# Expert results stored in token order, read back by plain loads, with the row loads on ScalarE's queue

## The reference, cut to what matters

```python
# first mixture: 8 experts, two per token
score = relu(x @ Wr1.T + br1) @ Wr2.T + br2
mask  = the two highest scores of each token;  w = softmax(where(mask, score, -inf))
out   = sum over e of w[e] * (relu(x @ W1[e].T + b1[e]) @ W2[e].T + b2[e])
# second mixture: 16 experts, two per token, and a shared expert
scores = softmax(x @ gate_w.T);  topw, topi = top_k(scores, 2)
h = silu(x @ w1[e].T) * (x @ w3[e].T) * comb[e];  y = sum over e of h @ w2[e].T
z = (silu(x @ sw1.T) * (x @ sw3.T)) @ sw2.T
```

## Time and profile before

| | |
|---|---|
| median of 3 runs | 1690.05 us (1690.01 to 1706.47) |
| the profiled execution | 1697.83 us, of which the span is 1696.1 us |
| busy share of the span | PE 80%, PEld 56%, DVE 45%, POOL 33%, ACT 31% |
| first mixture, first matmul to last | 662.4 to 883.6 us |
| second mixture, first matmul to last | 1352.3 to 1636.2 us |
| after the last matmul | 1636.2 to 1696.1 us |

### The profile page before, as it was taken

The page is one execution under the profiler, slowest core; times in us unless marked ns, Lnnn a source line. Parts: engine busy times, 40 slices in busy tenths (PEclk is TensorE's granted clock), DMA queues, the critical chain, the costliest instruction groups (busy, mean ns, idle before and its releaser), DMA issues.

```text
span 1696.1 us, 23482 instructions
## 1 busy us (share of the span) xinstructions
PE 1351.3 (80%) x7272; PEld 947.6 (56%) x7272; DVE 763.5 (45%) x1336; ACT 528.0 (31%) x894; POOL 560.4 (33%) x622
## 2 busy tenths in 40 slices
PE   0558799999998874999974778989899899999850
PEld 0223243443444453999972745747566588888850
DVE  1386689677786742111115545364444322222212
ACT  0354467677553210333320315043150100010100
POOL 5268789676674722101016000000003400101025
PEclk9968799899898876999996677888978999999985
DMA  5064264543543118888842000000000588888843
GB/s 129 19 155 117 53 165 124 130 100 88 155 116 76 41 41 252 271 276 271 277 147 70 5 1 1 1 0 0 1 1 31 155 242 227 229 239 226 231 109 95
DMA packets 71615, 206.45 MB, mean 122 GB/s; under 512 B 11360, under 2 KB 32608, under 8 KB 66752
## 3 DMA queue, kind: packets, MB, share of 16 engines
q1 hardware_dynamic: 59648, 181.28, 38.9%
q0 software_dynamic: 11904, 24.40, 5.0%
HBM read 183.42 MB, written 22.22 MB: 121 GB/s over the span
## 4 chain that ended last, share of the span: by engine, by line
PE 44%; DMA 16%; issue 10%; DVE 10%; POOL 8%; POOLq 5%; ACT 3%; DVEq 2%; SPq 2%; ACTq 1%
PE ps L927 31%; DMA expert<-arena 13%; PE ps L1299 3%; PE ps L1058 3%; DVE arena L1626 2%; POOL arena L633 2%; DMA arena<-sorted 2%; POOL ew_in L520 2%; PE ps L1072 2%; POOL ew_out L520 2%; PE ps L1088 1%; PE ps L1291 1%; POOL x_rows L387 1%; PE ps L922 1%; ACT arena L889 1%
## 5 line engine op out<-in xcount | busy, mean ns | idle before, releaser
L1626 DVE TENSOR_TENSOR_SCAN arena<-arena,ps 128x1024 f32<-128x1024 f32 x96 | 219.5, 2287 | 38.4 <-ACT arena L782 14.5
L927 PE MATMUL ps<-arena 96*128 96x128 f32 (+1 forms) x1680 | 222.5, 289 | 8.8 <-issue 8.2
L927 PEld LDWEIGHTS ps<-arena 96*128 96x128 f32 (+1 forms) x1680 | 213.6, 191 | 13.0 <-issue 12.9
L621 POOL DMA_DIRECT2D expert<-arena x88 | 47.7, 542 | 492.7 <-DVE arena L1752 272.7
L927 PE MATMUL ps<-xTF,wreg 96*128 96x512 f32 x352 | 199.3, 712 | 8.4 <-DVE arena L1792 4.6
L478 POOL DMA_INDIRECT sorted<-x_rows,row_i x64 | 62.7, 980 | 415.0 <-DVEq L1542 396.3
L927 PE MATMUL ps<-arena,ew_in 96*128 96x128 f32 x1248 | 149.9, 278 | 8.0 <-issue 7.7
L1058 PE MATMUL ps<-arena,pick 32*128 32x512 f32 x384 | 115.8, 691 | 48.5 <-DVE arena L1626 36.5
L927 PEld LDWEIGHTS ps<-arena,ew_in 96*128 96x128 f32 x1248 | 145.5, 194 | 11.9 <-issue 11.8
L927 PE MATMUL ps<-xT,wreg 96*128 96x512 f32 (+3 forms) x296 | 133.3, 599 | 7.5 <-DVEq L1807 5.4
L520 POOL TENSOR_TENSOR ew_in<-arena 128x1024 f32<-128x1024 f32 x48 | 112.6, 2353 | 68.6 <-PE ps L1072 41.2
(11 more groups left out here) (238 smaller groups left out, 1878.6 us busy)
## 6 DMA issues: line engine op xcount, KB each, us to landing
arena<-dt SPq DMA_DIRECT2D x64, 512.0 KB, 4.7
ew_in<-in_e_in SPq DMA_DIRECT2D x24, 768.0 KB, 6.4
arena<-in_e_in SPq DMA_DIRECT2D x24, 768.0 KB, 6.0
ew_in<-dt SPq DMA_DIRECT2D x32, 512.0 KB, 4.6
ew_out<-in_e_out SPq DMA_DIRECT2D x20, 675.0 KB, 6.7
arena<-in_e_out SPq DMA_DIRECT2D x20, 675.0 KB, 6.9
ew_in<-in_e_in SPq DMA_DIRECT2D x20, 576.0 KB, 5.5
arena<-in_e_in SPq DMA_DIRECT2D x20, 576.0 KB, 5.8
```

Of the source, the lines that this page charges most:

```text
L621: pool.dma_start(expert_rows[m][ds((i * 2 + k) * P, P), :], yb[k]).then_inc(s_yo[m][k], 16)
L927: last = pe.matmul(o, lhs, rhs, start=(n == 0), stop=(n == len(pairs) - 1))
L1626: ve.tensor_tensor_scan(hid[k % 3], dec[k % 3], bx.rearrange("p x t -> p (x t)"), 0.0, ALU.mult, ALU.add)\
```

## The change: what it does, and the diff

Each row that is scattered gets two more words: twice its token index plus 4, and its first place in the table (`x_all`, 194 words a row in place of 192). When a block's rows are loaded, VectorE works out for each of the 128 rows the row of a new table `token_rows` where its result belongs: the token's even row if this is its first place, its odd row if not, and row 2 or 3 for padding. GpSimd stores each result by an indirect DMA to those rows. It issues the stores of a pair one behind the other and then frees both buffers. The gathers go: SyncE loads each chunk of both results by one plain DMA (1536 bytes a token, 768 KB a chunk), the four directly one after the other, and signals VectorE through `s_ready`, which takes the place of `s_root` too.

The loads of a block's rows move from SyncE's list to ScalarE's (`load_row`, `first_rows`), where the two loads of the next pair stand ahead of this pair's relu or silu. SyncE waits for the scatters only after it has issued the weights of two blocks, and for the zeros not at all (ScalarE does). `route_blocks` works on 128 partitions instead of one, and its last part (`pos_i`) goes. The zeros and the blocks' first rows live in `pick`, so the memset of zeros now stands between the last scores and the last `route_picks`. GpSimd's loop over blocks is unrolled.

```diff
@@ expert_loads (SyncE)
                 sp.wait_ge(s_pos[m], 1)
-                sp.wait_ge(s_scat[m], 2 * B * 16)
-                sp.wait_ge(s_zero[m], (ne + 1) * 16)
-                with sp.Fori(0, nb // 4) as i:
+                def load_quad(i, first):
                     for j in range(4):
-                        k = j % 2
-                        sp.wait_ge(s_xbf[k], i * 2 + HALVES[m] + j // 2 + 1)
-                        sp.nop(nofuse=True)
-                        r = sp.value_load(rid[0:1, ds(i * 4 + j, 1)], min_val=0, max_val=ne * REG)
-                        sp.dma_start(xb[k], sorted_rows[m][ds(r, P), :]).then_inc(s_xb[k], 16)
+                        if first and j == 2:
+                            sp.wait_ge(s_scat[m], 2 * B * 16)
                         e = sp.value_load(eid[0:1, ds(i * 4 + j, 1)], min_val=0, max_val=ne - 1)
...
+            def token_loads(m, nb):
+                for k in range(2):
+                    sp.wait_ge(s_yo[m][k], 16 * (nb // 2))
+                for c in range(NCH):
+                    rows = token_rows[m][4 + 2 * c * CN:4 + 2 * (c + 1) * CN, :]
+                    sp.dma_start(both[:, c * CT:(c + 1) * CT, :].rearrange("p t (r d) -> p t r d", r=2),
+                                 rows.rearrange("(t p r) d -> p t r d", p=P, r=2)).then_inc(s_chunk[c], 16)
+                for c in range(NCH):
+                    sp.wait_ge(s_chunk[c], CHUNK_AT[c] + 16 * (m + 1))
+                    sp.sem_inc(s_ready, 1)
@@ scatter (GpSimd)
                 pool.wait_ge(s_row[m], n)
+                pool.tensor_scalar(x_all[:, t0:t0 + nt, D + 1:D + 2], row_f[:, 0, t0:t0 + nt]..., 0.0, None, ALU.add)
+                pool.drain()
@@ store_blocks (GpSimd); gather() goes
+                def issue(k, count):
+                    pool.wait_ge(s_yb[m], count)
+                    pool.indirect_dma_start(token_rows[m], bass.IndirectOffsetOnAxis(ids_i[k][:, 0:1], 0), yb[k], None)\
+                        .then_inc(s_yo[m][k], 16)
+                def release(k, count):
+                    pool.wait_ge(s_yo[m][k], count)
+                    pool.drain().then_inc(s_ybf[k], 1)
+                for i in range(nb // 2):
                     for k in range(2):
...
+                        issue(k, i * 2 + k + 1)
+                    for k in range(2):
+                        release(k, i * 16 + 16)
@@ ScalarE
+            def load_row(m, ne, b, k, turn):
+                act.wait_ge(s_xbf[k], turn)
+                act.nop(nofuse=True)
+                r = act.value_load(rid[0:1, b], min_val=0, max_val=ne * REG)
+                act.dma_start(xb[k], sorted_rows[m][ds(r, P), :]).then_inc(s_xb[k], 16)
+            def first_rows(m, ne):
+                act.wait_ge(s_pos[m], 1)
+                act.wait_ge(s_zero[m], (ne + 1) * 16)
+                act.wait_ge(s_scat[m], 2 * B * 16)
+                for k in range(2):
+                    load_row(m, ne, slice(k, k + 1), k, HALVES[m] + 1)
...
+            def silu_pair(i, more):
+                if more:
+                    for k in range(2):
+                        load_row(1, E1, ds(i * 2 + 2 + k, 1), k, i + HALVES[1] + 2)
                 for k in range(2):
                     act.wait_ge(s_bh[1], i * 2 + k + 1)
@@ VectorE
+            ve.memset(zero, 0.0)
             route_picks(0, E0, 3 * CT, CT)
...
+                ve.tensor_scalar(first_row[:, 0:nb], num, cst[:, C_IOTA:C_IOTA + 1], None, ALU.add)
...
+                        ve.scalar_tensor_tensor(out=ids[2 * h + k][:, :], in0=xb[k][:, D + 1:D + 2], scalar=first_row[:, ds(i * 4 + 2 * h + k, 1)],
+                                                in1=xb[k][:, D:D + 1], op0=ALU.not_equal, op1=ALU.add)
                         ve.drain().then_inc(s_xbf[k], 1)
...
                         ve.wait_ge(s_ybf[k], i * 2 + HALVES[m] + h + 1)
+                        ve.tensor_scalar(ids_i[k][:, :], ids[j][:, :], float(2 + k), None, ALU.max)
```

More of the change, by code:

```diff
@@ L69, in tower @@
         ps = ctx.enter_context(nc.psum_tensor("ps", [P, 8, 512], F32))
[L70 removed]
+        sorted_rows = [nc.dram_tensor(f"sorted{n}", (ne * REG + P, D + 2), F32, kind="Internal").ap() for n, ne in ((0, E0), (1, E1))]
         dt_rows = [nc.dram_tensor(f"dt{c}", (DG * 4, 2, 8, 2 * CN), F32, kind="Internal").ap() for c in range(NCH)]
[L72 removed]
+        token_rows = [nc.dram_tensor(f"token{n}", (2 * B * P + 4, D), F32, kind="Internal").ap() for n in range(2)]
         h_rows = sb("h_rows", [P, B, D])
[L76 removed]
+        x_all = sb("x_all", [P, B, D + 2])
+        x_rows = x_all[:, :, 0:D]
         tok_i = sb("tok_i", [P, B], I32)
@@ L145, in tower @@
         Ct = [part(23040 + 1024 * n, CN) for n in range(2)]
-        g1 = part(0, B * D).rearrange("p (t d) -> p t d", t=B)
-        g2 = part(B * D, B * D).rearrange("p (t d) -> p t d", t=B)
+        both = part(0, 2 * B * D).rearrange("p (t w) -> p t w", t=B)
         ar = mr
@@ L165, in tower @@
         QUADS, HALVES = (0, NB0 // 4), (0, NB0 // 2)
-        xb = [part(6144 + 256 * k, D) for k in range(2)]
+        xb = [part(6144 + 256 * k, D + 2) for k in range(2)]
         xbT = [part(6656 + 256 * k, 2 * P, KH).rearrange("p (k t) -> p k t", k=2) for k in range(2)]
@@ L178, in tower @@
         gate_w = sb("gate_w", [P, 2, B])
-        pos_i = sb("pos_i", [P, 2, B], I32)
+        ids = [sb(f"ids{k}", [P, 1]) for k in range(4)]
+        ids_i = [sb(f"ids_i{k}", [P, 1], I32) for k in range(2)]
         eid = sb("eid", [1, NB1], I32)
@@ L344, in expert_loads @@
                           .then_inc(s_w2[j], 16)
+                load_quad(0, True)
+                with sp.Fori(1, nb // 4) as i:
+                    load_quad(i, False)
             def store_dt(c, g):
@@ L860, in route_exp, with relu_quad @@
                 act.drain().then_inc(s_ex[m], 1)
+            def load_row(m, ne, b, k, turn):
[9 more added lines that the diff above has]
+                    load_row(m, ne, slice(k, k + 1), k, HALVES[m] + 1)
             route_exp(0, E0)
-            with act.Fori(0, NB0 // 4) as i:
+            first_rows(0, E0)
+            def relu_quad(i, more):
                 for j in range(4):
                     k, w = j % 2, e_out[0][j]
+                    if k == 0 and (more or j == 0):
+                        for n in range(2):
+                            load_row(0, E0, ds(i * 4 + j + 2 + n, 1), n, i * 2 + j // 2 + 2)
                     act.wait_ge(s_w2[j], i * 16 + 16)
@@ L871, in _ @@
                     act.drain().then_inc(s_ba[0], 1)
+            with act.Fori(0, NB0 // 4 - 1) as i:
+                relu_quad(i, True)
+            relu_quad(NB0 // 4 - 1, False)
             def shared_silu(i, f, banks):
@@ L914, in _ @@
                     act.drain().then_inc(s_bg, 1)
+            with act.Fori(0, NB1 // 2 - 1) as i:
+                silu_pair(i, True)
+            silu_pair(NB1 // 2 - 1, False)
         @block.tensor
@@ L1546, in route_blocks @@
                 ve.wait_ge(s_rank[m], n)
-                total, blocks, last, shift = rb(0, ne), rb(3, ne), rb(4, ne), rb(5, ne)
+                total, blocks, last = rb(0, ne), rb(3, ne), rb(4, ne)
                 over = rb(6, ne * B).rearrange("p (e t) -> p e t", e=ne)
@@ L1576, in route_blocks @@
                 ve.drain()
-                ve.tensor_scalar(rid[:, 0:nb], num, float(ne * REG), None, ALU.min)
+                ve.tensor_scalar(rid[:, 0:nb], num[0:1, :], float(ne * REG), None, ALU.min)
                 ve.drain().then_inc(s_pos[m], 1)
-                ve.tensor_tensor(shift, last, blocks, ALU.subtract)
+                ve.tensor_scalar(first_row[:, 0:nb], num, cst[:, C_IOTA:C_IOTA + 1], None, ALU.add)
                 ve.drain()
-                ve.scalar_tensor_tensor(out=shift, in0=shift, scalar=float(P), in1=cst[:, C_REG:C_REG + ne],
-                                        op0=ALU.mult, op1=ALU.subtract)
-                ve.drain()
-                moved = tiles_by(rb(6), 0, B, ne)
-                for r in range(2):
-                    ve.tensor_tensor(moved, tiles_by(hot_all[r][:, :], 0, B, ne),
-                                     shift.rearrange("p (a e) -> p a e", a=1).broadcast_to((P, B, ne)), ALU.mult)
-                    ve.drain()
-                    ve.tensor_reduce(rb(7, B), moved, AXX, ALU.add)
-                    ve.drain()
-                    ve.tensor_tensor(pos_i[:, r, :], rb(7, B), row_f[:, r, :], ALU.add)
-                    ve.drain()
             def route_weights(m, ne):
```

73 lines of the change are left out of this document (30 added, 43 removed).

## The result

The changed kernel takes 1646.48 us (median of 4 runs, 1641.61 to 1650.61) where the kernel before took 1692.24 beside it (4 runs, 1690.01 to 1706.47): ratio 0.9675, 95% interval 0.9625 to 0.9725 (the two medians divided give 0.973; the ratio on record weighs the runs another way). So 39 to 46 us are gained by the medians. The forecast was 61.8 of gain and 1628 us, range 1617 to 1650: right in direction, inside the range, some 18 us too good.

The account below looks back on a forecast made before the run. It took TensorE to bound the first mixture and nearly the second, and a queue of small steps the end. Terms 35.4 + 8.0 + 13 + 2.6 + 2.8 = 61.8 off 1690.05 gave 1628 us, range 1617 to 1650.

Parts of the forecast that it names:

- End: Last result to kernel end: plain chunk loads replace gathers, first sum 8.25 us after the copy; 35.4 us saved.
- middle: End of the first mixture: the same steps bring the sum forward, 8.0 us saved, bounds 0 and 9.4.
- Rival 1: The four chunk loads land together, not in turn: middle gains nothing, end 27.1, 1644.6 us; chance 0.12.
- Stores two at a time: Second mixture: paired stores leave TensorE setting the pace, 11.87 to 11.3 us a pair, 13 us saved.
- at most the 6.23: Second mixture: landing time in us of a pair's stores in flight together, within a GpSimd chain of about 9.
- Rival 2: Second mixture stays at 11.87 us a pair, held by weights, rows and indirect stores together: 1641.3 us; chance 0.15.
- Rows on ScalarE: Row loads moved to ScalarE: 2.6 us saved at the first mixture's start, 2.8 on later row loads.
- 655.1 + 4.95: First mixture's start: second row's issue time plus its landing time, giving 660.1, 1.8 us earlier.
- The lower bound written there: First mixture's start: 1.5 us lost if rows land only when both weight sets, 2.5 MB, have.
- The second mixture's start waits for the shared expert and gains nothing.: Second mixture's start: no gain from moving the row loads to ScalarE.
- ScalarE's own cost: Two row loads a pair, 2.8 us of about 11, expected covered; otherwise up to 2.8 us a pair added.
- Rival 3: Padding rows written to one of two rows take turns: 1745 us at 120 ns a write; chance 0.03.

Follow-up runs that it names:

- e8: Changed kernel with rows on SyncE, four row buffers, half a weight set ahead of first rows, VectorE writing the first place, last sums written out: 1633.33 us, ratio 0.9585.
- e11: The changed kernel itself, run again on another chip: 1663.56 us, ratio 0.9754.
- e10: Changed kernel with four row buffers on ScalarE and GpSimd's stores one by one: 1691.06 us, ratio 0.9950.
- e6: Changed kernel with four row buffers in place of two, still loaded by ScalarE: 1646.81 us, ratio 0.9661.
- e9: Kernel before with only the row loads moved to ScalarE and two weight sets early; stores one by one and gathers kept: 1702.19 us, ratio 0.9989.
- e5: Changed kernel with VectorE writing each row's first place, GpSimd's own operation and drain gone ahead of the scatter: 1651.21 us, ratio 0.9697.
- e7: Changed kernel with the eight removed VectorE operations for `pos_i` put back, their result unread: 1663.00 us, ratio 0.9787.
- e4: Changed kernel with 256 spare rows in place of two, so each padding row of a store has its own address: 1658.33 us, ratio 0.9725.
- e12: The e8 kernel run again, on the same chip as e11: 1626.38 us, ratio 0.9528.
- e3: Changed kernel with GpSimd waiting for each store and releasing its buffer before the next, still to token rows: 1688.78 us, ratio 0.9895.
- e1: Changed kernel with row loads back on SyncE in the old order, two buffers, no weight sets early: 1654.85 us, ratio 0.9732.

## Why the prediction was right and wrong

- *End, 35.4 forecast, 33.5 measured; middle, 8.0 and 8.0.* Right, with the path of the forecast: last store, chunk load, signal, 8.25 against 8.48 and 8.20. That it is so close is partly luck: the store landed in 3.27 us, not 2.3, while the wakes of GpSimd and SyncE took 0.28 and 0.06, not 0.5 each. Mis-sized: the sums, 3.2 each, come every 3.8. The 0.75 to 0.80 us between them, VectorE's loop step, had been hidden in the waits for gathers; e8, without the loop, has 3.06. Rival 1 (the chunk loads land together) is out.
- *Stores two at a time, 13 forecast.* The size was right where no row is late: the second mixture is 270.8 in e11, 13.1 under before, and e10 against e6 gives 12.2. In the first profile 4.9 was left; the late rows there account for the rest. Three sentences fell short. Stores in the first mixture "delay nobody that matters": so it was in the kernel before, where TensorE waits there for rows alone, but not once the row loads have moved (8.5 us of waiting in e9, 19.5 us in e10 against e6). The 11.87 was not the store chain's doing alone (e9). And a landing was to be "at most the 6.23": the median was 7.3, and 8 of 88 took over 9 us, which the forecast had named as a sign of being wrong; TensorE lost nothing by it that shows, other than through the rows. Rival 2, a pair held by the DMA engines together, did not come as such: e6 runs at 11.1 to 11.2 with the same bytes.
- *Rows on ScalarE, 2.6 + 2.8 forecast.* The step that failed is "655.1 + 4.95": the landing was taken from a row load that had one block's weights beside it. Beside those of four blocks, which nothing holds back any more, the loads in the chain took 10.08 and 12.93 us, and 10.99 inside the second mixture. The second row was also asked for 1.7 us later, counted from the last `row_i`, than the forecast had it, behind a zero store that took 3.42 us to land. The lower bound written there, 1.5 lost, was the right mechanism with two weight sets in place of four, and too small: 4.9 lost. Weights alone are not all of it: in e9, with its rows asked for 2.3 us sooner, the same move left the start at 23.7. What the first profile shows gained inside the first mixture, 4.3, was lost again in e11 (231.7). Alone the move gave nothing (e9). By the Trainium skill (DMA: Bandwidth & Descriptors, "Issuing engines are not separate DMA queues") that was to be expected: transfers interleave on the same engines whoever starts them. The trace agrees, with 10.99 us for a 97 KB row beside 1.5 MB of weights, and that sentence was set aside too lightly. (The sum by it is 57.7, not the 57.5 written there: 61.8 less 2.8 and 1.3.)
- *"The second mixture's start waits for the shared expert and gains nothing."* It lost 12.1, of which 5.7 is what the attention block ahead of it had gained; the two stages together went from 452.1 to 458.5, 6.4 lost. The steps missed: with the rows' issue no longer far ahead of TensorE, the scatter, the zeros and the rows' landing are next. GpSimd's small operation was costed as hidden by the zeros; in the first mixture it was (the chain has a zero store landing last, at 646.67), in the second the scatter ended later and e5 gained 5.3.
- *What was missed in all.* From the last `row_i` on the profile fell 22.5 us short of the forecast: 6.5 at the first start, 6.4 at attention and second start together, 8.1 in the second mixture, 1.9 at the end, less 0.5 in the first mixture.
- *"The old `pos_i` operations were off the path."* Wrong: e7 shows 3.1 us of waiting, and 4.2 us of the attention stage with the lower clock behind it. It went unseen in the total since the wait for rows came right behind.
- *ScalarE's own cost, nothing.* Nothing found against it: e6 has the same loads on ScalarE and both mixtures at TensorE's pace.
- *Rival 3, padding rows.* Out by e4. The Trainium skill (DMA: Bandwidth & Descriptors, "Rules for kernel authors") has each repeated index send its own write; whether they are sent singly no run here shows, but they cost nothing that shows.

Not tried: zeros issued from elsewhere. In e8 SyncE still spends 9.5 and 21.4 us on issuing them ahead of the first rows. Left open: what decides in a given run whether a row with two buffers comes late.

## What to carry to other kernels

A load that moves to another queue also lets go the queue that it leaves: ask what that one will now send, price the load by a row with that traffic beside it, and compare with the time that its buffers allow. If the two are close, add buffers before moving the load. Where an operation leaves the path, look at once for what arrives next there; a gain can be real and still end in the next wait.

## What the runs showed of the hardware beyond that

A late row costs more than its wait. The wait of 3.41 us at 1517.22 made that step 16.55 us in place of 11.2, 5.3 more, since the matmuls behind it ran at a lower clock (0.81 in that stretch). How long the wait is does not decide it alone: at the end of attention the same 16 matmuls took 7.13 us behind a wait of 2.25 (e5) and 10.44 behind one of 2.17 (e12).

Token-order stores land in 4.6 us one by one (e3, e10), about as a direct store of the same 96 KB (4.5): the scattered addresses cost nothing that shows. Two at a time they land in 7.3 (changed) and 7.1 (e6), but in e8, where the two of a pair are in flight together as well (issued 1.26 us apart), DMA issues show

```profile
token<-arena,ids_i POOLq DMA_INDIRECT x88, 4.6
```

and e12 has 4.5. So a second store in flight is not by itself what makes them slow. e8 and e12 have SyncE waiting for row buffers again; e1 has too, with two buffers, and its stores took 6.3. Which difference counts was not tried.
